# Learning rates folded into VectorE's products of the gradients, squares of the weights summed on ScalarE, and a new order of the chunk loop

## What is computed

```
gate = k @ w0;  hb = k @ w2;  sg = silu(gate);  hidden = sg * hb
dhidden = v @ w1.T;  dhbm = dhidden * sg;  dgate = dhidden * hb
dgba = silu_backprop(dgate, gate)
w1g = newtonschulz5((hidden * lr1).T @ v)
w0g = newtonschulz5((k * lr0).T @ dgba)
w2g = newtonschulz5((k * lr2).T @ dhbm)
w  = w + wg;  w = w / (norm of w over its rows + 1e-5) * first norm     (each of w0, w1, w2)
o  = silu(q @ w0) * (q @ w2) @ w1
```

## Time and profile before

| | us |
|---|---|
| median of three runs | 895.45 |
| lowest, highest | 894.72, 899.19 |
| profiled execution | 899.54 |
| its span | 897.8 |
| prologue and chunk 0 | to 75 |
| loop, 14 turns | 75 to 625 |
| chunk 15, experts | 625 to 897.8 |

### The profile page before, as it was taken

The page is one execution under the profiler, slowest core; times in us unless marked ns, Lnnn a source line. Parts: engine busy times, 40 slices in busy tenths (PEclk is TensorE's granted clock), DMA queues, the critical chain, the costliest instruction groups (busy, mean ns, idle before and its releaser), DMA issues.

```text
span 897.8 us, 16374 instructions
## 1 busy us (share of the span) xinstructions
PE 833.9 (93%) x4972; PEld 514.8 (57%) x4972; DVE 687.4 (77%) x2354; ACT 649.2 (72%) x1417; POOL 350.4 (39%) x324
## 2 busy tenths in 40 slices
PE   6999999999999999999999999998799999999994
PEld 3647576675757667575766757575555444444441
DVE  2798989898898989889898988989686554454441
ACT  2878988888888889889898988987485434444441
POOL 2324344444544444453444445344114232222222
PEclk9999999999999999999999999999899999999998
DMA  9776435161633517154251614438615465555450
GB/s 326 270 223 178 111 103 154 62 199 46 180 102 112 149 64 213 51 163 109 81 140 51 189 44 100 107 119 251 181 28 93 79 127 93 94 95 86 79 92 4
DMA packets 79126, 111.01 MB, mean 124 GB/s; under 512 B 14128, under 2 KB 35760, under 8 KB 78400
## 3 DMA queue, kind: packets, MB, share of 16 engines
q1 hardware_dynamic: 70720, 92.85, 36.7%
q0 software_dynamic: 8176, 16.85, 9.9%
q10 hardware_dynamic: 144, 0.26, 0.1%
HBM read 47.22 MB, written 64.55 MB: 124 GB/s over the span
## 4 chain that ended last, share of the span: by engine, by line
PE 63%; DVE 15%; ACT 8%; DMA 6%; issue 4%; POOL 3%; SPq 0%; DVEq 0%; POOLq 0%; ACTq 0%
PE bank L129 17%; PE bank L135 7%; PE bank L1060 7%; DMA out_x<-t_arena,t_tokx 4%; PE bank L1070 4%; POOL t_small L2871 2%; PE bank L613 2%; DVE t_small L1549 2%; PE bank L709 2%; ACT t_arena L2481 2%; PE bank L650 1%; PE bank L618 1%; PE bank L645 1%; PE bank L636 1%; DMA xs_scratch<-t_arena 1%
## 5 line engine op out<-in xcount | busy, mean ns | idle before, releaser
L129 PEld LDWEIGHTS bank<-t_arena 128*128 128x128 bf16 (+1 forms) x1536 | 123.2, 122 | 111.4 <-issue 30.5
L129 PE MATMUL bank<-t_arena 128*128 128x128 bf16 (+1 forms) x1536 | 156.1, 236 | 13.0 <-ACT t_arena L2490 6.4
L1060 PE MATMUL bank<-t_arena 128*128 x208 | 93.6, 593 | 0.0
L135 PE MATMUL bank<-t_ident,t_arena 128*128 128x128 f32 x398 | 65.5, 280 | 11.7 <-DVE t_arena L1105 6.2
L3027 POOL DMA_INDIRECT out_x<-t_arena,t_tokx x25 | 38.8, 1552 | 93.7 <-DMA out_x<-t_arena,t_tokx 77.3
L135 PEld LDWEIGHTS bank<-t_ident,t_arena 128*128 128x128 f32 x398 | 46.1, 142 | 45.6 <-issue 17.3
L2798 ACT ACTIVATE t_arena<-t_arena,t_small 128x128 f32<-128x128 f32 x100 | 41.1, 481 | 35.4 <-DVE t_tokx L2191 35.4
L2877 POOL TENSOR_TENSOR t_small<-t_small,t_half 128x8 f32<-128x8 f32 x14 | 24.5, 1748 | 103.5 <-DVE t_small L1549 103.5
L1060 PEld LDWEIGHTS bank<-t_arena 128*128 128x128 f32 x208 | 37.5, 190 | 37.3 <-issue 37.3
L129 PE MATMUL bank<-t_W,t_arena 128*128 128x128 f32 x384 | 54.8, 288 | 0.6 <-ACT t_W L2389 0.2
L1070 PE MATMUL bank<-t_arena 128*128 x108 | 50.8, 593 | 0.5 <-ACT t_arena L2793 0.5
(11 more groups left out here) (1121 smaller groups left out, 2406.9 us busy)
## 6 DMA issues: line engine op xcount, KB each, us to landing
xs_scratch<-t_arena SPq DMA_DIRECT2D x16, 2064.0 KB
t_arena<-xs_scratch SPq DMA_DIRECT2D x156, 64.0 KB
t_arena<-in_gate_up SPq DMA_DIRECT2D x32, 256.0 KB, 3.9
wm_scratch<-t_arena SPq DMA_DIRECT2D x30, 256.0 KB
t_arena<-in_wmod SPq DMA_DIRECT2D x5, 1024.0 KB, 10.4
t_arena<-in_down SPq DMA_DIRECT2D x16, 256.0 KB, 3.1
out_x<-t_arena SPq DMA_DIRECT2D x16, 256.0 KB, 2.1
t_arena<-wm_scratch SPq DMA_DIRECT2D x4, 1024.0 KB
```

The source lines that it names most:

```text
L129: mm = pe.matmul(bank[:, s], lhs[:, s], rhs[:, s], start=True, stop=True)
L135: mm = pe.transpose(bank[:, 128 * k:128 * k + 128], src[:, 128 * k:128 * k + 128], idn)
L1060: mm = pe.matmul(AA(u)[:, :], xT[u % 2][:, 128 * k:128 * k + 128], w_e[:, bass.ds(which[u], 1), 512 * k:512 * k + 512], start=(k == 0), st ...
```

## The change

- The scaled copies kl0, kl2 and vl go. TensorE multiplies the plain k (rk) and v (rv), which now have two buffers each by the parity of the chunk. The rates are multiplied into dhm (lr2), hid (lr1) and dgt (lr0) by folded: one scalar_tensor_tensor per head instead of one tensor_tensor of 512 columns. VectorE now waits for nothing from ScalarE's copies when it writes the rates, and dhm waits for the rates (written by VectorE itself).
- The squares of the new weights are summed by ScalarE as it squares (summed: one activation with accum_out per head), and the three reductions wr go. GpSimd's powers of the weights' norms wait for ScalarE.
- The copy osb goes: VectorE's product osb reads the output o from PSUM.
- The order of TensorE's, VectorE's and ScalarE's queues in the loop is new: among others hA before hid and dgt; ve before dhm; z12 and na12 behind x0 of n2 and osb; the rates' polynomial spread to the end of the turn; lr2's matmul later; AA and pieces of the projections between other steps of the chains; mg behind the transposes of the new w2, w0 and the rank matmuls, with only the transposes of w1 between it and the next gate. GpSimd's order is the same.
- In the prologue one element of next8 is set to -2048 by a memset, and chunk 0 and chunk 15 get folded and summed too.

The diff, cut to the helpers and, in the loop, TensorE's gradients and end of turn, VectorE's head, rates and end, ScalarE's and GpSimd's parts:

```diff
+        def summed(act, sums, x, to):
+            for h in range(H):
+                s = slice(128 * h, 128 * h + 128)
+                last_head = act.activation(to[:, s], x[:, s], ACT.Square, accum_out=sums[:, h:h + 1])
+            return last_head
+
+        def folded(dve, to, x, rate, y):
+            for h in range(H):
+                s = slice(128 * h, 128 * h + 128)
+                last_head = dve.scalar_tensor_tensor(out=to[:, s], in0=x[:, s], scalar=rate[:, h:h + 1], in1=y[:, s], op0=ALU.mult, op1=ALU.mult)
+            return last_head
...
                 pe.wait_ge(fwd_dve, nth(FWD_DVE, c, "dhm"))
                 pe.wait_ge(fwd_act, nth(FWD_ACT, c, "hbs"))
-                heads(pe, B2, kl2[c % 2], dhm).then_inc(n2_pe, 1)
+                heads(pe, B2, rk[c % 2], dhm).then_inc(n2_pe, 1)
...
+                heads(pe, B1, hid, rv[c % 2]).then_inc(n1_pe, 1)
...
+                pe.wait_ge(prep_act, nth(PREP_ACT, p, "raw1"))
+                turned(pe, P1, rk[p % 2], 4, ident[:, :]).then_inc(prep_pe, 1)
                 pe.wait_ge(apply_act, nth(APPLY_ACT, a, "lgT"))
                 pe.matmul(A0[:, 0:NE], lgT[:, :], selr[:, 0:NE], start=True, stop=True).then_inc(apply_pe, 1)
+                pe.wait_ge(prep_act, nth(PREP_ACT, p, "raw2"))
+                turned(pe, P2, rv[p % 2], 4, ident[:, :]).then_inc(prep_pe, 1)
+                pe.wait_ge(n2_dve, nth(N2_DVE, c, "WT"))
+                turned(pe, B2, WT[2], 4, ident[:, :]).then_inc(n2_pe, 1)
                 pe.wait_ge(prep_dve, nth(PREP_DVE, p, "tq"))
-                turned(pe, P0, raw[0], 4, ident[:, :]).then_inc(prep_pe, 1)
+                turned(pe, P0, raw0, 4, ident[:, :]).then_inc(prep_pe, 1)
+                pe.wait_ge(n0_dve, nth(N0_DVE, c, "WT"))
+                turned(pe, B0, WT[0], 4, ident[:, :]).then_inc(n0_pe, 1)
+                pe.wait_ge(apply_dve, nth(APPLY_DVE, a, "msk"))
+                if a == 0:
+                    pe.wait_ge(set_dve, nth(SET_DVE, 0, "onb"))
+                if a == 0:
+                    pe.wait_ge(set_dve, nth(SET_DVE, 0, "upb"))
+                pe.matmul(A0[:, 8:16], upperb[:, :], msk[:, :], start=True, stop=False)
+                pe.matmul(A0[:, 8:16], onesb[:, :], cum[a % 2][:, :], start=False, stop=True).then_inc(apply_pe, 1)
                 pe.wait_ge(prep_act, nth(PREP_ACT, min(c + 1, NC - 1), "kT"))
...
                     q = slice(32 * (e // 2), 32 * (e // 2) + 32)
                     mm = pe.matmul([P0, P1, P2][j][:, :], la[e % 2][q, 128 * k:128 * k + 128], lb[k // 4][q, :], start=True, stop=True)
                 mm.then_inc(mg_pe, 1)
-                pe.wait_ge(n0_dve, nth(N0_DVE, c, "WT"))
-                turned(pe, B0, WT[0], 4, ident[:, :]).then_inc(n0_pe, 1)
-                pe.wait_ge(n2_dve, nth(N2_DVE, c, "WT"))
-                turned(pe, B2, WT[2], 4, ident[:, :]).then_inc(n2_pe, 1)
-                pe.wait_ge(apply_dve, nth(APPLY_DVE, a, "msk"))
...
-                dve.wait_ge(fwd_act, nth(FWD_ACT, c, "sg"))
-                dve.wait_ge(fwd_pe, nth(FWD_PE, c, "dh"))
-                dve.tensor_tensor(dhm, B1[:, :], sg, ALU.mult).then_inc(fwd_dve, 1)
                 dve.wait_ge(s_x[p % 4],16 * (p // 4 + 1))
                 dve.bn_stats(bst, x1[:, p % 4, :]).then_inc(prep_dve, 1)
                 dve.wait_ge(prep_dve, nth(PREP_DVE, p, "bnst"))
                 dve.bn_aggr(mv[p % 2], bst).then_inc(prep_dve, 1)
-                dve.wait_ge(fwd_act, nth(FWD_ACT, c, "hbs"))
-                dve.tensor_tensor(hid, sg, hb, ALU.mult).then_inc(fwd_dve, 1)
                 dve.wait_ge(prep_dve, nth(PREP_DVE, p, "bnag"))
                 dve.tensor_scalar(rstd[p % 2], mv[p % 2][:, 1:2], LNEPS, None, ALU.add).then_inc(prep_dve, 1)
-                dve.wait_ge(fwd_dve, nth(FWD_DVE, c-1, "dgb"))
-                dve.tensor_tensor(dgt, B1[:, :], hb, ALU.mult).then_inc(fwd_dve, 1)
-                dve.wait_ge(fwd_act, nth(FWD_ACT, c, "tm"))
-                dve.scalar_tensor_tensor(out=pp, in0=sg, scalar=-1.0, in1=tg, op0=ALU.add, op1=ALU.mult).then_inc(fwd_dve, 1)
+                dve.wait_ge(fwd_act, nth(FWD_ACT, c, "sg"))
+                dve.wait_ge(fwd_pe, nth(FWD_PE, c, "dh"))
+                dve.wait_ge(rate_dve, nth(RATE_DVE, c, "lr"))
+                folded(dve, dhm, B1[:, :], lr12[c % 2][:, 8:12], sg).then_inc(fwd_dve, 1)
                 dve.wait_ge(prep_pool, nth(PREP_POOL, p, "rs"))
                 dve.wait_ge(prep_pe, nth(PREP_PE, p-1, "T"))
                 dve.tensor_scalar(hA, x1[:, p % 4, :], mv[p % 2][:, 0:1], rstd[p % 2], ALU.subtract, ALU.mult).then_inc(prep_dve, 1)
+                dve.wait_ge(fwd_act, nth(FWD_ACT, c, "hbs"))
+                folded(dve, hid, hb, lr12[c % 2][:, 4:8], sg).then_inc(fwd_dve, 1)
+                dve.wait_ge(fwd_dve, nth(FWD_DVE, c-1, "dgb"))
+                folded(dve, dgt, B1[:, :], lr12[c % 2][:, 0:4], hb).then_inc(fwd_dve, 1)
+                dve.wait_ge(fwd_act, nth(FWD_ACT, c, "tm"))
+                dve.scalar_tensor_tensor(out=pp, in0=sg, scalar=-1.0, in1=tg, op0=ALU.add, op1=ALU.mult).then_inc(fwd_dve, 1)
...
                 dve.tensor_tensor(NX[2], NZT[2], NZ[2], ALU.add).then_inc(n2_dve, 1)
+                dve.wait_ge(apply_pool, nth(APPLY_POOL, a, "orr"))
+                dve.tensor_tensor(h4(osb), h4(A0[:, :]), bc(orr), ALU.mult).then_inc(apply_dve, 1)
+                dve.wait_ge(rate_pe, nth(RATE_PE, p, "lr2"))
+                dve.tensor_tensor(z12, P0[:, 0:12], blr[:, :], ALU.add).then_inc(rate_dve, 1)
+                dve.wait_ge(rate_dve, nth(RATE_DVE, p, "z"))
+                dve.scalar_tensor_tensor(out=na12, in0=z12, scalar=-1.0, in1=z12, op0=ALU.mult, op1=ALU.min).then_inc(rate_dve, 1)
+                dve.wait_ge(n1_act, nth(N1_ACT, c, "NA0"))
+                dve.tensor_scalar(NAB[1], NA[1], NSB, None, ALU.mult).then_inc(n1_dve, 1)
                 dve.wait_ge(rate_pool, nth(RATE_POOL, p, "e"))
                 dve.tensor_scalar(s12, e12, 2.0, None, ALU.add).then_inc(rate_dve, 1)
...
-                dve.wait_ge(n2_act, nth(N2_ACT, c, "wq"))
-                dve.tensor_reduce(wss[2], h4(sq3[2]), AX, ALU.add).then_inc(n2_dve, 1)
...
-                dve.scalar_tensor_tensor(out=place(c, 1), in0=P1[:, :], scalar=2.0, in1=place(c, 1), op0=ALU.mult, op1=ALU.add).then_inc(mg_dve, 1)
+                dve.wait_ge(mg_pe, nth(MG_PE, c, "mg"))
+                dve.wait_ge(s_st[c % 4],48 * (c // 4 + 1))
+                dve.scalar_tensor_tensor(out=place(c, 2), in0=P2[:, :], scalar=2.0, in1=place(c, 2), op0=ALU.mult, op1=ALU.add).then_inc(mg_dve, 1)
                 dve.tensor_reduce(posf, po[:, :, :], AX, ALU.add).then_inc(apply_dve, 1)
                 dve.wait_ge(apply_dve, nth(APPLY_DVE, a, "w1"))
                 dve.tensor_tensor(h2x[:, 514:515], es, h2x[:, 515:516], ALU.subtract).then_inc(apply_dve, 1)
+                dve.scalar_tensor_tensor(out=place(c, 1), in0=P1[:, :], scalar=2.0, in1=place(c, 1), op0=ALU.mult, op1=ALU.add).then_inc(mg_dve, 1)
                 dve.wait_ge(apply_dve, nth(APPLY_DVE, a, "pr"))
                 dve.tensor_copy(posu[a % 2][:, :], posf).then_inc(apply_dve, 1)
                 dve.scalar_tensor_tensor(out=place(c, 0), in0=P0[:, :], scalar=2.0, in1=place(c, 0), op0=ALU.mult, op1=ALU.add).then_inc(mg_dve, 1)
...
-                act.activation(sq3[2], WT[2][:, :], ACT.Square).then_inc(n2_act, 1)
+                summed(act, wss[2], WT[2], sq3[2]).then_inc(n2_act, 1)
...
-                act.copy(osb, A0[:, :]).then_inc(apply_act, 1)
...
-                act.wait_ge(rate_dve, nth(RATE_DVE, p, "lr"))
-                act.wait_ge(prep_dve, nth(PREP_DVE, p, "tk"))
-                act.wait_ge(n2_pe, nth(N2_PE, p-2, "G"))
-                for h in range(H):
-                    s = slice(128 * h, 128 * h + 128)
-                    row = act.activation(kl2[p % 2][:, s], raw[1][:, s], ACT.Identity, scale=lr12[p % 2][:, 8 + h:9 + h])
-                row.then_inc(prep_act, 1)
-                act.wait_ge(n0_pe, nth(N0_PE, p-2, "G"))
-                for h in range(H):
-                    s = slice(128 * h, 128 * h + 128)
-                    row = act.activation(kl0[p % 2][:, s], raw[1][:, s], ACT.Identity, scale=lr12[p % 2][:, 0 + h:1 + h])
-                row.then_inc(prep_act, 1)
...
-                pool.wait_ge(n2_dve, nth(N2_DVE, c, "wr"))
+                pool.wait_ge(n2_act, nth(N2_ACT, c, "wq"))
```

494 lines of the change are left out of this document (203 added, 291 removed).

## The result

| | before | after |
|---|---|---|
| median | 895.09 us (4 runs) | 932.93 us (4 runs) |
| lowest, highest | 894.65, 899.19 | 931.37, 934.67 |
| profiled execution, its span | 899.54, 897.8 | 934.67, 932.9 |

The changed kernel takes 1.041 times as long (95% interval 1.0389 to 1.0431), 37.8 us more by the medians. The forecast was 929.8, in a range of 885 to 950.

A forecast was written before the change was run, and what follows sets the result against it. TensorE is busy 93% of the span; with three engines over 85% busy, queue order decides. Terms +2.0 + 0.55 - 0.25 + 0.15 = +2.45 a chunk, times 14 = +34.3 us, on the median 929.8; range 885 to 950.

The forecast's parts named there:

- The step that decides: VectorE's hA before hid and dgt waits for rs behind POOL's scatters; G1 and G0 come 2.0 us a chunk later.
- called safe: G2 on TensorE: dhm ends at gate + 3.6, before G2 starts at 3.69, so no delay.
- The rate exponent: VectorE idles some 2.3 us before s12 for POOL's e12; BX0 of n1 +0.55 us a chunk, bounds 0 and 1.6.
- e12: POOL's 12-column power, 2.47 us in the kernel before; VectorE's s12 waits for it, standing still some 2.3 us.
- The rest: Waits for L1490 and L2490 go, A1 of n1 waits 0.6: together -0.25 us a chunk; Th2 stretch +0.05.
- The seam: Stretch from Th2 to the next gate: 9.8 us against 9.72, +0.1 a chunk.
- ScalarE's sums: Each weight's squares with sums take 1.18 us instead of 0.52, +2.0 a chunk in all; ScalarE still gains 2.0.
- VectorE's busy time: Three reductions go (-1.8 us), split products add 1.2 a chunk: net -0.6.
- B: Slack elsewhere takes up the delay, G1 only 0.9 us later, sum 0 a chunk: 895 us; chance 0.08.
- C: Faster: hA has no wait because rs is done by gate + 3.5; -1.2 us a chunk, 878.7; chance 0.20.
- E: Squares with sums cost 1.63, norms late, +1.4 us on ScalarE, half on the seam: 939; 0.60 together with main forecast.
- D: TensorE's idle 2 us before G1 brings the clock to 0.50 once every chunk: 18 us more, 948; chance 0.08.

The follow-up runs named there:

- Run 1: Changed kernel with hA moved back behind pp, nothing else moved: 912.56 us, 1.0184 times before.
- run 4: Changed kernel with VectorE's cast of the positions (posu) placed ahead of u1 instead of behind it: 923.57 us, 1.0314 times before.
- run 10: Changed kernel, hA left in place, next chunk's row statistics ahead of u2 and rs ahead of GpSimd's two scatters: 915.38 us, 1.022 times before.
- run 9: On run 3: ScalarE scales v by lr1, hid is one 512-column product again, the variance's two small operations go behind dhm: 887.01 us, 0.9907 times before.
- run 2: Changed kernel with s12 moved behind the steps of n1 and n2, directly ahead of its reciprocal: 919.96 us, 1.0271 times before.
- Run 8: On run 3: first term of n0's second factor ahead of a row statistic, scales of new w0 and w1 ahead of the router's small operations: 907.67 us.
- Run 6: Kernel before, in its own order, with ScalarE's sums of squares replacing VectorE's three reductions, scaled copies kept: 929.01 us, 1.0384 times before.
- run 3: Changed kernel with both hA back behind pp and s12 directly ahead of its reciprocal: 898.57 us, 1.0031 times before.

## Why the prediction was right

Step by step, in us a turn, from the timelines of one turn of each kernel (the earlier trace rows and above):

| | predicted | measured |
|---|---|---|
| G1, G0 behind the gate | +2.0 | +2.16 (6.97 to 9.13) |
| BX0 of n1, beyond that | +0.55 | +0.73 (20.86 to 23.75, less 2.16) |
| to Th2, beyond that | -0.20 | +0.32 (29.31 to 32.52, less 2.89) |
| Th2 to the next gate | +0.10 | -0.38 (9.73 to 9.35) |
| sum | +2.45 | +2.83 |

**The step that decides** held. Predicted: cast done at gate + 1.17, rs at 4.92, hA at 4.95, G1 at 7.55. Measured: 1.21, 4.91, 4.95, 7.73. Run 1 shows the price by undoing it, run 4 by moving the cast, run 10 by taking the scatters out of the way. The folded group costs 1.05 from start to start (370.89 to 371.94), against the 1.0 taken and within its bounds, 0.84 and 1.16. That holds both for hid, all of whose inputs are in SBUF, and for dgt, which reads PSUM. Of the prediction's estimates by the Trainium skill, VectorE: DVE Perf Modes, section The TRN2 errata (0.78 and 1.03), only the second fits. The idle time before hA was 1.05 instead of 1.4, because one detail was wrong: G2 was called safe. The statistics stand ahead of dhm now, which starts at gate + 2.77 instead of 2.51, and G2 starts at 3.95 instead of 3.69. This cost nothing by itself in the changed kernel, where rs came later anyway; run 9 shows that such time counts once hA's wait is gone.

The prediction took the 3.10 from the cast to the end of the second scatter for the same in all 14 turns; it is in twelve, and 3.89 and 3.19 in the first and the last.

Undoing that step gives back 1.44, not 2.16: in run 1 G0 starts at gate + 7.69, against 9.13 and, before, 6.97. The other 0.7 is, by the timelines, what the folded groups cost more, with the statistics ahead of dhm, and the old place of hA doesn't avoid it. Run 9 takes 0.65 of it away.

**The rate exponent** had the right mechanism and idle time (2.17 against 2.3), and where it was measured, at BX0 of n1, it came to +0.73 against +0.55. Its two parts were both too large, though, and offset each other. The walk took 1.6 for the stand before s12; run 2 gives back 1.02. Against that it set x0 of n2, which was to come 1 us sooner, and it did (1.3: gate + 17.38 before, 18.23 after, less the 2.16 by which all is shifted), but little of this reaches BX0. In run 2, where the stand is gone, ScalarE's copy behind BX0 starts at gate + 25.47, against 23.47 before, which is 0.2 sooner once the 2.2 of the shift is taken off. Behind x0 stands osb, for which VectorE now waits 0.4 for the power of the output norm, in each turn:

```profile
DVE t_arena L1497 <- POOL t_small L2805: 5.4, 14, 0.4
```

This puts off z12, na12 and so e12; the prediction had no such wait. How much of the gain it eats wasn't tried.

**The rest** was wrong in sign, for one wait. What the prediction walked is there: BX0 of n2 waits no more for L1490, the projection between A1 and AA1 of n0 fills the wait for L2490, and A1 of n1 waits for its own copy instead, 0.45 (L2448) against 0.6. What it had not is that BX1 of n0 waits 0.54 for L1573, VectorE's sum of two terms, and this is the size of the error (+0.32 against -0.20). Run 8 tried an earlier place for one of the two terms and found 0.07, so what makes L1573 late stays open.

**The seam** was predicted too long by half a microsecond. TensorE waits 0.80 for the new w0, which the prediction named as the risk, but nothing at mg, and this is the larger. The cast comes at 1.21, as walked.

**ScalarE's sums** cost what was taken: four activations with a sum run from 396.38 to 397.56, 1.18. Each of the four leaves two records:

```profile
396.38 0.31 ACT L259 ACTIVATE t_arena<-t_WT 128x128 f32<-128x128 f32 x1
396.59 0.19 ACT L259 ACTIVATION_READ_ACCUMULATOR t_arena<-t_WT 128x1 f32 x1
396.69 0.30 ACT L259 ACTIVATE t_arena<-t_WT 128x128 f32<-128x128 f32 x1
```

ScalarE is busy for 1.84 less a turn (34.34 to 32.50), 2.0 predicted. Run 6 is what this term hid: the same work costs 1.2 a turn at full clock if the sums stand before the copies that TensorE waits for. The prediction said that only what TensorE waits for counts, and found the new order safe, which it is; it is not safe in general.

**VectorE's busy time** was to fall by 0.6 a turn and rose by 0.80 (35.04 to 35.84). The groups and the reductions are nearly as priced; the rest of the rise lies in the other instructions, whose records overlap less in the new order. The term had no place in the sum, so this cost the forecast nothing.

**In all**, 13 periods give 34.3, as the sum for 14 turns did with 2.45. The profiled turn gives 2.83, which would be 36.8 over 13 turns. The loop as a whole shows less because the kernel before had turns above its 39.04, 3.2 us in all (two stretches at half clock and the one turn of 39.60), and the changed one only 0.7 above its 41.87. The errors of the four rows, +0.16, +0.18, +0.52 and -0.48, offset one another in part, as do the two parts of the second row: the mechanism of the largest term was right, and the closeness of the time was in part luck. Of the rivals, B (slack takes it up) falls with the period of 41.87 and with run 3, where the two placements add to the hundredth; C (faster) with hA at 4.95; E with 1.18 for a group of sums; D (the clock) didn't happen here, with a wait of 1.72 before G1 in every turn and a half-clock stretch in one, but did in run 6.

## What to carry to other kernels

Moving one instruction up an in-order queue costs everything behind it the time it then waits, so follow its input back through the other engine's queue, to the instruction that stands ahead of it there (here two scatters and their index), before it is moved. Where three engines are over 85% busy, place a long small-tensor power so that VectorE has work of its own length to do until it is done, and keep independent small operations between dependent ones. Splitting one wide operation into four to fold a scalar in moves work from an engine with room to the one that is waited for; fold only the product whose time nobody waits for.
